# Stacked q and k transposed by fp32r matmuls, and one transpose for a group's negated maxima

## The reference

```python
# block 1: retention. 16 heads of 8 channels
q, k, v = proj(layernorm(x)); q, k = rotary(q), rotary(k)
qk = (q @ k.T) / sqrt(8) * decay_mask        # causal, per head
x = x + groupnorm(qk @ v) @ Wo.T
# block 2: attention and four experts, on h = layernorm(x)
h = rms(z, n1_w)
q, k, v = rms(heads(h @ wq.T), qn_w), rms(heads(h @ wk.T), kn_w), heads(h @ wv.T)
attn = softmax(where(causal, q @ k.T * 8 ** -0.5, -inf))
z = z + (attn @ v @ wo.T, first 32 channels zeroed)
moe = top-2-of-4 gated sum of four MLPs on rms(z, n2_w), first 32 channels zeroed
x = x + z + moe
```

## Time and profile before

| | |
|---|---|
| median of three runs | 1057.93 us |
| span of the profiled execution | 1055.9 us |
| TensorE matmul (PE) busy | 82% |
| TensorE weight loads (PEld) busy | 47% |
| VectorE (DVE) busy | 65% |
| ScalarE (ACT) busy | 49% |
| GpSimd (POOL) busy | 16% |
| mean granted TensorE clock | 0.904 |
| DMA traffic | 31.58 MB, mean 30 GB/s |

### The profile page before, as it was taken

One profiled execution on the slowest core, in us unless ns is written; L12 is line 12 of the kernel. 1 busy time (PEld: TensorE's weight loads), 2 busy tenths in 40 slices (PEclk: granted clock), 3 DMA queues, 4 the chain that ended last, 5 costly groups with the idle time before them and its releaser, 6 DMA issues.

```text
span 1055.9 us, 16178 instructions
## 1 busy us (share of the span) xinstructions
PE 870.4 (82%) x4609; PEld 501.0 (47%) x4656; DVE 683.5 (65%) x1824; ACT 518.3 (49%) x1080; POOL 171.3 (16%) x218
## 2 busy tenths in 40 slices
PE   2546898799879897798987998798977989879967
PEld 1424454364435554364543654355543644436434
DVE  5468836887368854788358873688557883578431
ACT  1213563456544574455644565455744556444634
POOL 5310202022010301022020210103010220202002
PEclk9676998899979998899988999799988999889989
DMA  4101110030100301021100301003010211003000
GB/s 142 40 11 33 38 41 12 1 74 9 41 11 3 78 10 41 0 50 31 40 11 0 80 1 40 11 6 75 16 35 0 53 28 40 1 0 81 2 1 10
DMA packets 30965, 31.58 MB, mean 30 GB/s; under 512 B 8768, under 2 KB 19136, under 8 KB 30912
## 3 DMA queue, kind: packets, MB, share of 16 engines
q1 hardware_dynamic: 26688, 28.93, 12.1%
q10 hardware_dynamic: 4224, 2.10, 0.7%
HBM read 5.58 MB, written 2.10 MB: 7 GB/s over the span
## 4 chain that ended last, share of the span: by engine, by line
PE 68%; DVE 19%; issue 6%; ACT 5%; DMA 1%; SPq 0%; DVEq 0%; POOL 0%; ACTq 0%; POOLq 0%
PE ring L589 9%; PE side L624 9%; PE outs L556 8%; DVE mxp L1053 6%; PE side L661 6%; PE ring L434 5%; PE ring L576 5%; PE single L434 4%; PE ring L445 4%; PE side L434 3%; PE side L639 3%; PE outs L456 3%; PE ring L592 2%; PE ring L536 2%; PE single L505 2%
## 5 line engine op out<-in xcount | busy, mean ns | idle before, releaser
L1053 DVE TENSOR_REDUCE mxp<-ring 128x4 f32<-128x512 f32 x320 | 204.9, 685 | 35.3 <-PE ring L576 31.1
L784 ACT ACTIVATE p<-ring 128x512 f32<-128x512 f32 x320 | 173.8, 602 | 67.0 <-PE ring L592 41.2
L589 PE MATMUL ring<-qx,ks 128*128 128x512 f32 x320 | 143.4, 499 | 18.8 <-DVE mxp L1053 17.2
L576 PE MATMUL ring<-kx,qs 128*128 128x512 f32 x320 | 144.1, 499 | 2.8 <-DVE mxp L1053 0.4
L1153 POOL TENSOR_SCALAR_AFFINE_SELECT p<-p 128x512 f32<-128x512 f32 x64 | 39.6, 635 | 315.4 <-ACT p L693 314.5
L589 PEld LDWEIGHTS ring<-qx,ks 128*128 128x128 f32 x320 | 62.6, 201 | 57.5 <-DVE mxp L1053 26.6
L556 PE MATMUL outs<-p,v 128*32 128x512 f32 (+3 forms) x1024 | 87.6, 442 | 0.8
L1048 DVE COPY oT<-outs 128x512 f32<-128x512 f32 x32 | 22.1, 689 | 89.4 <-PE outs L556 89.4
L576 PEld LDWEIGHTS ring<-kx,qs 128*128 128x128 f32 x320 | 62.5, 199 | 35.4 <-DVE mxp L1053 23.1
L434 PE MATMUL single<-sb_t_id,nat 128*128 128x128 f32 x128 | 28.3, 361 | 60.3 <-DVE nat L1081 29.5
L661 PE MATMUL side<-sb_w_dn,h 128*128 128x96 f32 x384 | 52.2, 276 | 6.0 <-ACT h L812 6.0
(11 more groups left out here) (168 smaller groups left out, 1615.8 us busy)
## 6 DMA issues: line engine op xcount, KB each, us to landing
qx<-qs SPq DMA_DIRECT2D x32, 256.0 KB, 4.7
qx<-qs SPq DMA_DIRECT2D x32, 192.0 KB, 3.8
kx<-ks SPq DMA_DIRECT2D x96, 64.0 KB, 2.0
x_in<-x_dram ACTq DMA_DIRECT2D x8, 256.0 KB, 3.3
qx<-qs SPq DMA_DIRECT2D x32, 64.0 KB, 2.0
qx<-h SPq DMA_DIRECT2D x128, 2.0 KB, 1.7
out_dram<-yout SPq DMA_DIRECT2D x8, 256.0 KB, 2.3
sb_t_cos<-t_cos_dram SPq DMA_DIRECT2D x1, 512.0 KB, 5.2
```

What stands on the lines that cost most here:

```text
L576: last = nc.tensor.matmul(dst[:, :], qs[:, g, qt * 128:(qt + 1) * 128], kx[:, g % 2, :, kt * 128:(kt + 1) * 128], start=True, stop=kt < qt)
L589: last = nc.tensor.matmul(dst[:, :], ks[:, g, kt * 128:(kt + 1) * 128], qx[:, g, :, qt * 128:(qt + 1) * 128], start=True, stop=kt < qt)
L784: A_(p2(kt)[:, :, (qt - kt) * 128:(qt - kt + 1) * 128], pr[(U_AB + at) % 4][:, :].rearrange("p (j n) -> p j n", j=J), ACT.Exp, scale=float ...
L1053: V.tensor_reduce(mxp[:, qt, :, kt], ring(b, U_AB + at)[:].rearrange("p (j n) -> p j n", j=J), AX.X, ALU.max).then_inc(max_read, 1)
```

## The change

`stacked` no longer uses fp32 transposes: each of the four becomes an ordinary matmul whose stationary operand is the 128x128 piece of `stack` as fp32r and whose moving operand is an fp32r identity `idr` of 128 columns. `idr` is a new constant, cast by VectorE in `ready`. The negated maxima are stored as (head, tile) instead of (tile, head), so that one transpose of 16 columns gives a 16x128 result instead of four of 4 columns that give 4x512. The copy to `mT` and the source of the shift DMA follow: each DMA now reads four partitions of 128 numbers.

```diff
--- before.py
+++ after.py
@@ -67,7 +67,7 @@
 
 FFN_AT = {"start": (0,), "scored": (1,), "weighed": (2,), "spread": (3,), "projected": (4, 5), "normed": (6, 7)}
 LEAD_EARLY = {"start": -1, "weighed": 0, "projected": 1}
-LEAD_STEPS, FRONT_STEPS, TAIL_STEPS, BACK_STEPS, N_CONSTS = 14, 44, 20, 15, 8
+LEAD_STEPS, FRONT_STEPS, TAIL_STEPS, BACK_STEPS, N_CONSTS = 14, 44, 20, 15, 9
 
 
 def tables():
@@ -124,6 +124,7 @@
         cos_t = ww["t_cos"][:].rearrange("p (t c) -> p t c", t=NT)
         sin_t = ww["t_sin"][:].rearrange("p (t c) -> p t c", t=NT)
         idb = sb("idb", [128, 128], bf16)
+        idr = sb("idr", [128, 128], f32r)
         negb = sb("negb", [128, J, 128], bf16)
         negkb = sb("negkb", [128, J, 128], bf16)
         wqk = sb("wqk", [128, D])
@@ -174,7 +175,7 @@
         x1 = sb("x1", [128, NT, C])
         z = sb("z", [128, NT, C])
         mxp = sb("mxp", [128, NT, J, NT])
-        mneg = sb("mneg", [128, G, NT, J])
+        mneg = sb("mneg", [128, G, J, NT])
         rcp = sb("rcp", [128, NT, H])
         xfT = sb("xfT", [128, T])
         gl = sb("gl", [128, 8, NT, E])
@@ -191,7 +192,7 @@
         h3 = sb("h3", [128, 2, T])
         sil = hB
 
-        mT = h3[0:J, :, :].bitcast(f32r)
+        mT = h3[0:J * NT, :, 0:128].bitcast(f32r)
         halved = lambda ap: ap[:].rearrange("p a (b c) -> p (a b) c", b=2)
         raw, cosp, sinp = halved(h1), halved(hA), halved(hB)
         qT = h0[:, 0, :]
@@ -436,8 +437,11 @@
 
             def stacked(dst, s, g):
 
-                return transposed(dst, lambda t: stack[:, s, t, J * g:J * g + J, :]
-                                  .rearrange("p j s -> p (j s)").bitcast(f32))
+                for t in range(NT):
+                    last = nc.tensor.matmul(dst[:, t * 128:(t + 1) * 128],
+                                            stack[:, s, t, J * g:J * g + J, :].rearrange("p j s -> p (j s)"), idr[:],
+                                            start=True, stop=True)
+                return last
 
             def scores(b, t):
                 for g in range(G):
@@ -595,7 +599,8 @@
                         gm = MT_AT[at]
                         single(b, S_MT + gm)
                         pe.wait_ge(mneg_ready, count(mneg_ready, b, gm + 1))
-                        transposed(ps[0:J, :], lambda t: mneg[:, gm, t, :]).then_inc(single_filled, 1)
+                        nc.tensor.transpose(ps[0:J * NT, 0:128], mneg[:, gm].rearrange("p j t -> p (j t)"), ident[:])\
+                            .then_inc(single_filled, 1)
                     for g_kt in WEIGH_AT.get(at, []):
                         weigh(*g_kt)
                     beside(at, side)
@@ -792,7 +797,7 @@
                         if gm >= 2:
 
                             act.wait_ge(shift_ready[gm % 2], count(shift_ready[gm % 2], b, J * 16))
-                        A_(mT[:, gm % 2, :], ps[0:J, :], ACT.Copy).then_inc(mT_ready, 1)
+                        A_(mT[:, gm % 2, :], ps[0:J * NT, 0:128], ACT.Copy).then_inc(mT_ready, 1)
                     beside(at, side)
                 act.wait_ge(single_filled, count(single_filled, b, S_AO + 1))
                 A_(chT[:, :], ps[:, :], ACT.Copy).then_inc(aoT_ready, 1)
@@ -1057,7 +1062,7 @@
                             dve.wait_ge(max_read, count(max_read, b, NU * (g + 1)))
                             go(V.tensor_reduce(mxm[:].rearrange("p t j -> p (t j)"), mxp[:].rearrange("p t j k -> p (t j) k"),
                                                AX.X, ALU.max))
-                            V.tensor_scalar(mneg[:, g], mxm[:], -1.0, None, ALU.mult).then_inc(mneg_ready, 1)
+                            V.tensor_scalar(mneg[:, g].rearrange("p j t -> p t j"), mxm[:], -1.0, None, ALU.mult).then_inc(mneg_ready, 1)
                     if OT_AT.get(at) == 0 and not first(b):
 
                         dve.wait_ge(out_ready, count(out_ready, b, 0))
@@ -1127,6 +1132,7 @@
             def ready():
                 dve.wait_ge(loaded, 16 * (len(ww) - len(PROJECTION + ROTATION)))
                 V.tensor_copy(idb[:], ident[:]).then_inc(consts_ready, 1)
+                V.tensor_copy(idr[:], ident[:]).then_inc(consts_ready, 1)
                 V.tensor_copy(negb[:], neg32[:].unsqueeze(1).broadcast_to([128, J, 128])).then_inc(consts_ready, 1)
                 V.tensor_scalar(negkb[:], tri[:].unsqueeze(1).broadcast_to([128, J, 128]), 1.0, -NEG, ALU.subtract, ALU.mult)
                 V.tensor_tensor(wqk[:], ww["w_qk"][:, 0:D], ww["w_qk"][:, D:2 * D], ALU.mult).then_inc(consts_ready, 1)
@@ -1253,7 +1259,7 @@
                 sp.wait_ge(qx_ready, count(qx_ready, b, 12 * 16))
                 for j in range(J):
                     sp.dma_start(qx[32 * j + SHIFT:32 * j + SHIFT + 1, g, j, :].bitcast(f32),
-                                 mT[j:j + 1, g % 2, :].bitcast(f32)).then_inc(shift_ready[g % 2], 16)
+                                 mT[NT * j:NT * j + NT, g % 2, :].bitcast(f32)).then_inc(shift_ready[g % 2], 16)
 
             def lead(b, part):
                 if part == RET:
```

## The result

The changed kernel took 1050.99 us in the median of four runs (1049.23 to 1053.13) against 1057.91 us (1057.64 to 1057.99) before: a ratio of 0.9943 with an interval of [0.9926, 0.996], some 6.9 us faster. The profiled execution is one of the slower ones of the four, 1052.72 us with a span of 1050.9. Of the runs on other chips that follow, two of the kernel before (1655.76 and 2049.88 us) and one of e11 (2773.15 us) were far slower than the rest and are left out of the ratios.

What follows compares the result with a forecast made beforehand. TensorE was taken as busiest (82%), with clock returns fixing a 122.88 us period; -0.65 + 0.2 = -0.45 us per batch settles at 0.6 once, taken as 0.5: 1057.93 - 0.5 = 1057.4 us, range 1053.0 to 1061.0.

Steps and rivals of the forecast that it cites:

- The cut in the maxima's transposes: Negated maxima: three fewer transposes save 0.33 us of PE per group; only groups 2 and 3 count, 0.65 us per batch.
- ACT's copy: Copy of the transposed maxima, 0.58 us, gets shorter; counted as nothing, at best 0.3 us for each of two groups.
- The stacked matmuls: Stacked q and k: bound by weight load, 0.111 us each against 0.109; +0.2 us per batch, from +0.1 to +0.5.
- not one pass: Rival: stacked fp32r matmuls stream in four passes, 0.23 us each, 8.2 us more per batch, 1118 us; 10 in 100.
- weights load fast: Rival: stacked matmuls' weights load at streaming rate, 3.5 us less PE per batch, 1034 us; 5 in 100.
- The sum per batch: Whole batch: -0.65 for the maxima plus 0.2 for the stacking gives -0.45 us per batch.
- The shift rows: Shift DMAs read four partitions; landing of 1.7 us at worst doubles, covered before a group's first exponent matmul.
- The clock in batch 0: Stacking stretch of batch 0: with half the streaming the clock could return to 2.4 GHz later, but this is damped away.
- A quarter kept, and the gain once and not eight times: Batch period of 122.88 us: each batch keeps a quarter of a displacement, so the advance settles at 0.6 us, once.
- The halving that was to explain the quarter: Returns from 1.2 to 2.4 GHz: work early by e ends ahead by e/2; two returns per batch leave a quarter.
- the clock does not pin the period: Rival: clock returns move with the work, each batch keeps its 0.45 us, 3.6 us in all, 1054.3 us; 22 in 100.
- The clock falls earlier in the maxima stretch: Rival: thinner PE work drops the clock before 485.3, losing 0.4 us per batch, some 2.8 us, about 1060.7; 13 in 100.

Runs made afterwards that it cites:

- e11: Kernel before with only the lead's eight stacking units as fp32r matmuls, maxima still transposed in four parts; ratio 1.0008.
- e3: Kernel before with the negated maxima's part alone, plus three unread transposes per group given back; 1056.55 us, ratio 1.0.
- e7: Changed kernel with the front part's nine stacking units back to fp32 transposes; 1048.4 us, ratio 0.9918 of the kernel before.
- e2: Kernel before with the fp32r stacking matmuls and `idr` alone, maxima unchanged; 1057.85 us, ratio 1.0009.
- e5: The changed kernel itself, run again on another chip beside the kernel before; 1051.03 us, ratio 0.9942.
- e6: Changed kernel with the lead's eight stacking units, in the attention part, back to fp32 transposes; 1056.36 us, ratio 0.9997 of the kernel before.
- e8: Changed kernel with three unread transposes of maxima given back per group; 1057.31 us, ratio 1.0003 of the kernel before.
- e17: Changed kernel with unread bf16 matmuls at four places where PE waits; 1028.68 us, ratio 0.9741 of the kernel before.
- e1: Kernel before with the negated maxima's part of the change alone, stacking still by fp32 transposes; 1056.34 us, ratio 0.9996.
- e16: Kernel before with unread bf16 matmuls at four places where PE waits; 1029.65 us, ratio 0.9745.

## Why the prediction was wrong, point by point

**The cut in the maxima's transposes**: right. 0.44 us of the chain became 0.11, twice per batch; the 16 columns of weights cost nothing that can be seen. ACT's copy got 0.32 us shorter, and it was right to count it at zero: the second group of exponent steps takes 11.48 us in e3 as before.

**The stacked matmuls**: right. The lead's 32 add 0.18 us to the second group of exponent steps (e11 11.66, before 11.48), the front's add nothing in a steady batch (25.2 us from the addition to the first maximum in both kernels), against +0.2 in the sum. They start 0.112 us apart, where the prediction had 0.111 and the transposes 0.109. The rivals "not one pass" (0.23 apart) and "weights load fast" (0.057) fall with that number. By the rule of the Trainium skill that the prediction weighed ("TensorE: Matmul & The Clock Gate", "Weight-path perf modes"), 128 weights of a type that isn't FP32 load fast; the 209 ns of L441, against 0.096 us for the bf16 identity, say that fp32r counts as FP32.

**The sum per batch**: right in place and nearly in size, 0.45 against 0.55 us measured where the clock does not fall.

**The shift rows**: in the steady batches of both kernels the first exponent matmul starts 0.73 to 0.74 us after the start, and 0.05 to 0.06 after the end, of the maximum that frees its ring buffer. So it waits for VectorE there, and nothing of the DMAs showed. The profile gives no landing time for them after.

**The clock in batch 0**: it does come back later there, as said, but in the changed kernel this isn't damped away. The stretch of the earlier trace rows after the change (columns as the earlier trace rows):

```profile
94.10:97.40 3.30, 3.30 (x18) 3.30 (x17) 2.14 (x4) 2.27 (x4) 0.00 (x0) 0.50 0.00 0
...
98.00:104.30 6.30, 6.30 (x21) 4.73 (x22) 3.96 (x7) 1.19 (x2) 0.00 (x0) 0.50 0.33 70
104.50:107.00 2.50, 2.38 (x12) 1.31 (x10) 2.50 (x6) 0.00 (x0) 0.00 (x0) 1.00 1.00 220
```

and in e7, where these units are transposes again:

```profile
94.50:97.80 3.30, 3.30 (x18) 3.30 (x17) 2.11 (x4) 2.27 (x4) 0.00 (x0) 0.50 0.00 0
97.95:101.30 3.35, 3.35 (x22) 2.49 (x22) 2.87 (x5) 1.19 (x2) 0.00 (x0) 0.99 0.34 81
```

Both fill PE with eighteen instructions of the same length, 3.30 of 3.30 us. After transposes the clock is back at 2.4 GHz before 98, after fp32r matmuls only by 104.5. It is so in every run: in the six kernels with fp32r matmuls in the front part (after, e2, e5, e6, e8, e17) this return lies between 103.2 and 104.7 us, in the other twelve between 95.6 and 98.8. The front part of batch 0, from the first addition to the first maximum, takes 27.2 us in e7, 29.1 in the changed kernel and 30.2 in e5. In the profiled executions of e5 and e7 the first interval differs by 3.0 us and the six that follow by 0.2 in their sum, so the 2.6 us between e5 and e7 are put down to batch 0. This isn't shown to be all: against the changed kernel's first trace, 1.4 us of e7's lead lie in the first interval and 2.0 in the six later ones. Where the period is pinned the same matmuls cost nothing: e6, which has them, is at 0.9997 and e1, which has not, at 0.9996.

**A quarter kept, and the gain once and not eight times**: this step failed. The sum let the advance settle at 0.6 us, took 0.5 of it, once, and forecast 1057.4; measured were 6.9 us. The four intervals of the earlier trace rows do converge, and e1, with 0.65 us less, converges too (122.0, 122.77, 122.87), so a pin is real. The wrong inference was that it acts on a displacement of any size. It was read from four delays of less than 0.5 us and then used for an advance that is renewed in every batch. The runs show that it holds at doses of +0.65, 0 and -0.65 us and not at -0.22 and -0.44. Where it fails, the batches do not settle. Their length creeps up from one to the next (122.1, 122.6, 123.1) until the clock doesn't fall at one place and returns earlier at another, which gives a batch of 120.3 us, and the row starts again. That makes 0.85 us per batch, seven or eight times, and not 0.5 once. The halving that was to explain the quarter isn't shown either. Besides 491.0 and 545.6 there is a third return in each batch, here at 566.1 us of the kernel before (columns as the earlier trace rows), and three halvings would keep an eighth:

```profile
559.30:566.10 6.80, 4.68 (x15) 3.28 (x16) 5.21 (x23) 1.13 (x2) 0.61 (x1) 0.50 0.00 0
566.20:569.60 3.40, 3.40 (x10) 1.31 (x8) 2.76 (x19) 1.19 (x2) 0.00 (x0) 1.00 0.00 0
```

**The rivals**: "the clock does not pin the period" was right in kind and had 22 in 100, but its size was wrong in the same way. It paid each batch its own gain of 0.45, 3.6 us in all, and took no account of stretches at 1.2 GHz that vanish in some batches; 0.85 per batch is nearly twice as much. 1054.3 us was 3.3 us too high, and with it the range's lower end. "The clock falls earlier in the maxima stretch" is what e1 does and what the batch of 123.1 us of the changed kernel does (13.4 us for its exponent steps); in e1 it brings the time back to that of before and no further.

**What stays open**: which doses are pinned, and whether a row repeats after two, three or four batches, could be found by running, not worked out beforehand. "Pinned" is read from one trace of each kernel. The rows tell that a fall or a return lies at one place or another, and that 0.2 us of work ahead of it moves it. I have no rule from the runs that gives the next place. The time of the kernel before also moves by 3.6 us from run to run on other chips (1054.8 to 1058.4) where it moved by 0.4 on the first; this was not followed up.

## What to carry to other kernels

Before a gain is summed up, look at the granted clock in two or three steady batches: if it falls at the same places in each, a few tenths of a microsecond of TensorE work may be worth nothing or several times its length, and only a run tells which. Try a dose on both sides before an edit is kept or dropped, and test its parts together as well as alone. Where TensorE waits and the clock falls after the wait, unread matmuls that end before the wait does can be worth more than trimming the work; here 34 of them per batch gave 2.5% alone (e16), and 2.6% together with the change (e17). Look at more than two intervals, since lengths that differ may repeat in threes or fours.

## What the runs showed of the hardware

A matmul of 128 fp32r columns with weights of 128 columns comes 0.112 us after the one before at 2.4 GHz, as weight loads of 128 fp32 columns do elsewhere (0.111), and so is worth no more than the fp32 transpose at 0.109.

Fp32 transposes bring the clock back where fp32r matmuls of 128 columns, as long and as dense, do not yet: 2.4 GHz before 98 us in e7 and at 98.5 before the change, against 104.5 after it. The same holds earlier in batch 0 for the lead's units: before the change the clock is at 2.4 GHz from 43.9 to 47.2, after it (fence below) it stays at 0.50 from 29.3 to 53.2. All eight kernels with the matmuls in the lead stay at 0.50 there for 23.9 us, and in the ten with transposes there the clock is back after 10.2 to 13.7 us.

```profile
29.40:53.10 23.70, 16.66 (x64) 13.17 (x64) 8.41 (x15) 7.86 (x12) 6.87 (x7) 0.50 0.20 44
```

The Trainium skill says ("TensorE: Matmul & The Clock Gate", "Part 4: PE-mode transpose") that the full clock doesn't engage for transposes, which do not count as a busy TensorE in the same way; it gives its times for bf16. For the fp32 transposes here these rows speak against it: the clock goes to 1.00 behind 3.30 us filled with them.

The shift DMAs move the same 2 KB each. From one partition they took more packets than from four. The page's line on DMA, first before and then after:

```profile
DMA packets 30965, 31.58 MB, mean 30 GB/s; under 512 B 8768, under 2 KB 19136, under 8 KB 30912
```

```profile
DMA packets 27893, 31.57 MB, mean 30 GB/s; under 512 B 5184, under 2 KB 16064, under 8 KB 27840
```

3072 fewer for 128 DMAs, 24 for each. Those under 512 bytes fell by 3584, 28 for each DMA, and those from 512 to 2048 bytes rose by 512, four for each. The counts are the same in e1, so the DMAs' part of the change alone makes the difference. It changed no time here.
